# A graph message passing on one core: a slot pair's sum added in two halves instead of in one piece

## The chip, the core and the metric

The kernel runs on one core of a Trainium2 chip. The metric is the device time of one execution in microseconds; for each kernel several runs are timed and their median is given. The engines are named as the profile names them: PE (TensorE, with PEld for its weight loads), DVE (VectorE), ACT (ScalarE), POOL (GpSimd) and SP (SyncE, which here only issues transfers). "q" behind a name (DVEq) is the engine's queue.

## What is computed

A network of two layers on 1250 nodes with 512 features, each layer a message passing over 20000 edges followed by a block with attention and expert or plain feed-forward parts. The change lies in the message passing of the second layer. Cut to what matters:

```python
x0, x1 = lin(node_feats)                     # 128 scalars and 128 vectors of 3 a node
h = three layers of silu on edge_feats       # 64 values an edge
w1, w2, w3, w4 = split(h @ W_mlp4 / 8, 4)    # 4 x 128 weights an edge
s0, s1 = x0[sender], x1[sender]
p1 = w1 * s0 * y0                            # y0, y1: the edge's attributes
p2 = (w2 * s0)[:, :, None] * y1[:, None, :]
p3 = w3[:, :, None] * s1 * y0[:, None, :]
p4 = w4 * einsum('eum,em->eu', s1, y1) / SQRT3
msg0 = segment_sum(concat([p1, p4]), receiver, num_nodes)
msg1 = segment_sum(concat([p2, p3]), receiver, num_nodes)
out = lin(msg0, msg1) / 10
```

An edge's message has 1024 values (p1 and p3: 4 x 128, with the factor y0; p2 and p4: 4 x 128). The sum over the edges of a receiving node is what the changed lines add up.

## The kernel before

The program is a row of stages. Each stage (`stage`, L70) runs one block for each engine and ends in a barrier of all engines. The stage of interest is the first of `graph_sum1` (L2150), which runs from about 1362 to 1787 us of the span; the stage behind it turns `acc` and multiplies it with the output weights.

The edges are sorted by receiver into 176 slots of 128 edges (NS1), so that the two slots of a pair (88 pairs, PAIRS) belong to the same tile of 125 nodes. Which tile that is stands in `tile_base`, and is read at run time. `acc` (`g_acc`) holds 10 tiles of 1024 columns in SBUF.

For each slot, numbered i, j, t or s after the step at which an engine takes it:

- SP loads `h` (`g_h`) for 16 slots at a time, three buffers. POOL gathers the sending nodes' rows (`got`, L2208, 10 buffers) and makes `plain`, the 0/1 matrix of edge against receiver (L2216, 6 buffers), when `summed` says that PE is done with the slot six before. Once, in its step 9, POOL clears `acc` (L2219).
- PE makes the weights w1 to w4 of slot s in PSUM (`pw`, L2234, two matmuls).
- ACT makes the first part of the dot product (L2264), `hot` = `plain` times y0 (L2272) and three of the message's eight parts (L2281, signals `made_scaled`). `hot` has 4 buffers (MR), so L2272 for slot i waits for `summed` of slot i-4.
- DVE makes the rest: L2295 and L2310 (dot product, slot s), L2304, L2314, L2318 (message, slot s-1). `msg` has 4 buffers as well; L2302 and L2303 wait for `summed` and `made_scaled` of the slot four before.
- PE sums slot t = s-4 over the receivers: L2245 multiplies `hot` with the message's first 512 columns, L2248 `plain` with the other 512. Each is float32 and shows as two passes with a weight load each. The first slot of a pair opens two PSUM banks of `pm`, the second adds to them and closes them, and `summed` counts the slots done. `pm` has four banks, so two pairs are in flight.
- DVE adds a closed pair to its tile of `acc`: in every second step it reads the tile's number (L2323, `value_load`), waits for `summed` (L2324) and for its own last add (L2328), and adds the 1024 columns of two banks in one instruction (L2330), which signals `added`.
- Before a pair q opens its banks, PE waits at L2244 until pair q-2 is added.

Each engine works through its instructions in the order of the program; in a step s of DVE that order is L2295 (s), L2304 (s-1), L2310 (s), L2314 and L2318 (s-1), and in odd steps from 7 on L2330 for pair (s-7)/2. In a step s of PE it is L2234 (s), L2245 and L2248 (s-4).

The first message passing (`graph_sum0`'s loop in `first_layer`) has an add of the same kind, L1578: 125x512 from PSUM into a slice whose place is read at run time, with the making of a `hot` tile (L1566) behind it.

Of the kernel before, what the change touches and what calls it, by code (L numbers as in the profile page):

```python
# [22 lines left out]
ALU = mybir.AluOpType  # L23
# [4 lines left out]
D = 512  # L28
TN = 125
# [6 lines left out]
PAIRS = (E + NT * (2 * TE - 1)) // (2 * TE)  # L36
NS1 = 2 * PAIRS
# [2112 lines left out]
def graph_sum1(nc, c, table_d, tile_base, nodes_d, h_d, w4_d, out0_d, out1_d, x):  # L2150
# [4 lines left out]
    with ExitStack() as ctx:  # L2155
        sb = lambda name, shape, dt=F32: ctx.enter_context(nc.sbuf_tensor(f"{name}_{nc.next_id()}", shape, dt))
        acc = sb("g1_acc", [TN, NT, 2 * D])
        wo = sb("g1_wo", [128, 2, 2, 128])
        with ExitStack() as inner:
# [11 lines left out]
            pm = inner.enter_context(nc.psum_tensor(f"g1_pm_{nc.next_id()}", [128, 4, 512], F32))  # L2171
            table = table_d.rearrange("(p t) c -> p t c", p=128)
            with stage(nc, "edges_in", "w4_in", "w4_high", "w4_low", "wo_in", "zeroed", "made_plain", "made_hot", "weighed",
# [5 lines left out]
                @block.sync  # L2179
                def _(sp):  # L2180
                    def load(g):
                        if g >= HR:

                            sp.wait_ge(weighed, G1E * (g - HR + 1))
                        sp.dma_start(h[:, g % HR, :].bitcast(F32), h_d[g, :, :]).then_inc(h_in[g % HR], 16)

                    sp.dma_start(edges[:, :, :], table).then_inc(edges_in, 16)
                    for n in range(2):
                        sp.dma_start(w4[64 * n:64 * n + 64, :], w4_d).then_inc(w4_in, 16)
                    for g in range(HR):  # L2190
                        load(g)
                    for n in range(2):
                        sp.dma_start(wo[:, 0, n, :], out0_d[128 * n:128 * n + 128, :]).then_inc(wo_in, 16)
                        sp.dma_start(wo[:, 1, n, :], out1_d[128 * n:128 * n + 128, :]).then_inc(wo_in, 16)
                    for g in range(HR, GROUPS):
                        load(g)
                    sp.wait_ge(wo_in, 64)
# [23 lines left out]
                @block.tensor  # L2221
                def _(pe):
                    pe.wait_ge(w4_high, 1)
                    pe.wait_ge(w4_low, 1)
                    for s in range(NS1 + 4):
                        if s < NS1:
                            g, r = s // G1E, s % G1E
                            if r == 0:
                                pe.wait_ge(h_in[g % HR], 16 * (g // HR + 1))
                            if s >= 4:  # L2230

                                pe.wait_ge(made_msg, s - 3)
                            for n in range(2):
                                ins = pe.matmul(pw[:, s % 4, :], h[:, g % HR, TE * r:TE * r + TE], w4_two[:, n, :],  # L2234
                                                start=(n == 0), stop=(n == 1))
                            ins.then_inc(weighed, 1)
                        t = s - 4
                        if t < 0:
                            continue
                        q, second = t // 2, t % 2  # L2240
                        pe.wait_ge(made_hot, t + 1)
                        pe.wait_ge(made_msg, t + 1)
                        if q >= 2 and not second:
                            pe.wait_ge(added, q - 1)  # L2244
                        pe.matmul(pm[0:TN, 2 * (q % 2), :], hot[:, t % MR, :],  # L2245
                                  msg[:, t % MR, 0:4, :].rearrange("p a b -> p (a b)"), start=not second, stop=bool(second))
                        pe.wait_ge(made_scaled, t + 1)
                        pe.matmul(pm[0:TN, 2 * (q % 2) + 1, :], plain[:, t % OR, :],  # L2248
                                  msg[:, t % MR, 4:8, :].rearrange("p a b -> p (a b)"), start=not second, stop=bool(second))\
                            .then_inc(summed, 1)  # L2250
# [34 lines left out]
                @block.vector  # L2285
                def _(dve):
                    dve.wait_ge(w4_high, 1)
                    dve.tensor_tensor(w4_two[:, 1, :], w4[:, :], w4_two[:, 0, :].bitcast(F32), ALU.subtract)\
                        .then_inc(w4_low, 1)
                    dve.wait_ge(edges_in, 16)  # L2290
                    for s in range(NS1 + 7):
                        i = s
                        if i < NS1:
                            dve.wait_ge(dot0, i + 1)
                            dve.scalar_tensor_tensor(dot[:, i % MR, :], got[:, i % GR, 256:384], edges[:, i, 6:7],  # L2295
                                                     dot[:, i % MR, :], ALU.mult, ALU.add).then_inc(dot1, 1)
                        i = s - 1
                        if 0 <= i < NS1:
                            dve.wait_ge(weighed, i + 1)
                            if i >= MR:  # L2300

                                dve.wait_ge(summed, i - MR + 1)  # L2302
                                dve.wait_ge(made_scaled, i - MR + 1)  # L2303
                            dve.tensor_tensor(msg[:, i % MR, 0::8, :], pw[:, i % 4, 0:256].rearrange("p (a u) -> p a u", a=2),  # L2304
                                              got[:, i % GR, 0:128].unsqueeze(1).to_broadcast((128, 2, 128)), ALU.mult)\
                                .then_inc(made_own, 1)
                        i = s
                        if i < NS1:
                            dve.wait_ge(dot1, i + 1)
                            dve.scalar_tensor_tensor(dot[:, i % MR, :], got[:, i % GR, 384:512], edges[:, i, 7:8],  # L2310
                                                     dot[:, i % MR, :], ALU.mult, ALU.add).then_inc(dot2, 1)
                        i = s - 1
                        if 0 <= i < NS1:
                            dve.tensor_tensor(msg[:, i % MR, 1:4, :],  # L2314
                                              pw[:, i % 4, 256:384].unsqueeze(1).to_broadcast((128, 3, 128)),
                                              got[:, i % GR, 128:512].rearrange("p (m u) -> p m u", m=3), ALU.mult)
                            dve.wait_ge(dot2, i + 1)
                            dve.tensor_tensor(msg[:, i % MR, 7, :], pw[:, i % 4, 384:512], dot[:, i % MR, :], ALU.mult)\  # L2318
                                .then_inc(made_msg, 1)
                        t = s - 6  # L2320
                        if t >= 0 and t % 2:
                            q = t // 2
                            at = dve.value_load(tile_base[0:1, q:q + 1], min_val=0, max_val=NT - 1)  # L2323
                            dve.wait_ge(summed, t + 1)  # L2324
                            if q == 0:
                                dve.wait_ge(zeroed, 1)
                            else:
                                dve.wait_ge(added, q)  # L2328
                            dst = acc[:, bass.ds(at, 1), :].rearrange("p a b -> p (a b)")
                            dve.tensor_tensor(dst, dst, pm[0:TN, 2 * (q % 2):2 * (q % 2) + 2, :].rearrange("p a b -> p (a b)"),  # L2330
                                              ALU.add).then_inc(added, 1)
                    dve.wait_ge(added, PAIRS)

        acc_t = sb("g1_acct", [128, 2, 8, TN])
        p8 = ctx.enter_context(nc.psum_tensor(f"g1_pt_{nc.next_id()}", [128, 4, 512], F32))
# [218 lines left out]
```

## Time and profile before

| | |
|---|---|
| median of 3 runs | 3323.68 us (3322.3 to 3328.46) |
| the profiled execution | 3329.74 us, span 3327.9 us |
| mean granted clock of TensorE | 0.949 |
| PE busy, share of the span | 2957.0 us, 89% |
| DVE busy, share of the span | 2030.3 us, 61% |
| ACT busy, share of the span | 1465.1 us, 44% |
| POOL busy, share of the span | 944.3 us, 28% |

The profiled execution is one run; its span goes from the first to the last instruction, and its own time is 1.8 us longer. Shares of busy time are means over all stages. Matmul records carry modelled ends and overlap each other, so PE's starts tell more than its busy time. In a timeline, the bracket behind a row gives the idle time of that engine just before and the event that came last before the start.

### The profile page before, as it was taken

The numbers are of one execution on the slowest core, as the hardware profiler recorded it, in microseconds if no ns is written. First come the engines' busy times: TensorE is split into PE (matmuls) and PEld (weight loads), VectorE is DVE, ScalarE is ACT, GpSimd is POOL, SyncE is SP. The second block draws the span as 40 slices with busy tenths as digits, with TensorE's granted clock in tenths as the row PEclk, the third lists the DMA queues.
The fourth block names the chain that finished last, engine by engine and source line by source line (L and its number), as shares of the span: only waits on it lengthen the run. The fifth ranks groups of instructions, "written<-read, shape, count | busy, mean of one in ns | idle before, by whom it ended". The sixth has DMA issues, their size and how long they took to land. (4 is left out here: it accounts for less than half of the span.)

```text
span 3327.9 us, 47565 instructions
## 1 busy us (share of the span) xinstructions
PE 2957.0 (89%) x15718; PEld 2057.7 (62%) x15718; DVE 2030.3 (61%) x4335; ACT 1465.1 (44%) x3160; POOL 944.3 (28%) x994
## 2 busy tenths in 40 slices
PE   5978789998589968699998888989999899998898
PEld 3522287776557644244445665568777687776787
DVE  8989746776421126599996345652777537776444
ACT  1000035665135426466664345533666436664322
POOL 2057664671134330566661000000000000001210
PEclk9999999999689979799999899989999999999899
DMA  3047765331559953544441453226431154311322
GB/s 99 13 142 206 199 154 133 63 74 41 166 179 341 340 172 141 195 137 140 137 126 57 162 143 77 50 68 189 87 71 25 25 189 91 79 25 39 104 82 82
DMA packets 222607, 402.70 MB, mean 121 GB/s; under 512 B 44222, under 2 KB 140626, under 8 KB 218526
## 3 DMA queue, kind: packets, MB, share of 16 engines
q1 hardware_dynamic: 170866, 262.09, 27.7%
q0 software_dynamic: 49744, 134.92, 14.6%
q10 hardware_dynamic: 1756, 2.64, 0.3%
q8 instruction: 130, 2.13, 0.3%
q14 instruction: 111, 0.91, 0.1%
HBM read 315.84 MB, written 87.71 MB: 121 GB/s over the span
## 5 line engine op out<-in xcount | busy, mean ns | idle before, releaser
L904 ACT ACTIVATE at_p<-at_pb,at_max 125x1250 f32<-125x1250 f32 (+4 forms) x320 | 383.8, 1199 | 301.9 <-DVE at_unused L975 273.5
L790 PE MATMUL at_pb<-ident,at_p 125*125 125x125 f32 x2880 | 433.0, 281 | 20.0 <-ACT at_p L904 17.0
L790 PEld LDWEIGHTS at_pb<-ident,at_p 125*125 125x125 f32 x2880 | 390.2, 190 | 83.0 <-ACT at_p L904 22.3
L807 PE MATMUL at_pb<-at_pt,at_v 125*64 125x250 f32 x2880 | 355.7, 384 | 5.2 <-DVE s_t L1008 3.0
L968 DVE TENSOR_REDUCE at_wide<-at_pb 125x1 f32<-125x1024 f32 x240 | 293.6, 1224 | 21.0 <-PE at_pb L773 2.7
L890 ACT ACTIVATE at_pt<-at_pb 125x500 f32<-125x500 f32 (+1 forms) x448 | 232.8, 520 | 96.3 <-PE at_pb L790 91.9
L807 PEld LDWEIGHTS at_pb<-at_pt,at_v 125*64 125x64 f32 x2880 | 188.6, 137 | 104.0 <-issue 14.4
L750 PE MATMUL at_pb<-at_s,at_shared 128*128 128x500 f32 (+1 forms) x1152 | 229.3, 361 | 23.4 <-ACT at_shared L852 23.4
L986 DVE COPY at_pt<-at_pb 125x500 f32<-125x500 f32 (+1 forms) x416 | 232.3, 582 | 21.6 <-PE at_pb L790 21.6
L975 DVE TENSOR_SCALAR_CACHE_REDUCE at_unused<-at_pb,at_wide 125x226 bf16<-125x226 f32 x240 | 107.8, 449 | 204.7 <-PE at_pb L773 201.7
L750 PEld LDWEIGHTS at_pb<-at_s,at_shared 128*128 128x128 f32 x1152 | 196.0, 194 | 56.4 <-ACT at_shared L852 24.2
L712 POOL TENSOR_TENSOR s_t<-s_t,at_all 128x500 f32<-128x500 f32 (+1 forms) x33 | 42.9, 1300 | 648.8 <-DVE s_t L1008 648.6
L695 POOL DMA_INDIRECT table<-rows,slots x160 | 198.2, 1239 | 96.5 <-issue 87.5
L1452 PE MATMUL so_ps<-g_got,g_hot 128*125 128x512 f32 x332 | 177.5, 637 | 46.3 <-issue 11.9
L2208 POOL DMA_INDIRECT g_got<-nodes,g_edges x176 | 176.8, 1005 | 134.7 <-DMA g_edges<-table 104.4
L1404 POOL DMA_INDIRECT g_got<-support,so_ids x166 | 161.5, 973 | 149.8 <-DVE so_ids L1532 98.1
L2234 PE MATMUL g_pw<-g_w4two,g_h 128*128 128x512 f32 x352 | 182.1, 601 | 22.3 <-DMA g_h<-h_edges 18.5
L2245 PE MATMUL g_pm<-g_msg,g_hot 128*125 128x512 f32 x352 | 188.3, 617 | 14.9 <-DVE g_acc L2330 7.8
L771 PE MATMUL at_pb<-at_kh,at_q 128*125 128x512 f32 (+5 forms) x448 | 178.4, 405 | 19.5 <-ACT at_p L904 17.7
L2248 PE MATMUL g_pm<-g_msg,g_plain 128*125 128x512 f32 x352 | 181.5, 597 | 0.0
L771 PE MATMUL at_pb<-at_shared 128*125 128x512 f32 (+5 forms) x448 | 177.5, 403 | 3.3 <-ACT at_p L904 2.6
L1881 DVE COPY mo_y<-mo_py 78x512 f32<-78x512 f32 x64 | 44.0, 687 | 213.7 <-PE mo_py L1849 148.4
(336 smaller groups left out, 5695.1 us busy)
## 6 DMA issues: line engine op xcount, KB each, us to landing
w_ring<-in_L_ffn_w SPq DMA_DIRECT2D x128, 512.0 KB, 11.5
at_shared<-k_parts SPq DMA_DIRECT2D x64, 312.5 KB
ml_w<-in_mlp_w SPq DMA_DIRECT2D x64, 256.0 KB
k_parts<-at_shared SPq DMA_DIRECT2D x64, 250.0 KB, 2.9
q_parts<-at_shared SPq DMA_DIRECT2D x64, 250.0 KB, 2.8
h_edges<-em_both SPq DMA_DIRECT2D x11, 1024.0 KB, 4.1
g_h<-h_edges SPq DMA_DIRECT2D x11, 1024.0 KB, 5.7
at_shared<-q_parts SPq DMA_DIRECT2D x32, 312.5 KB
```

Source lines behind the costliest of these rows:

```text
L695: pool.indirect_dma_start(table_d, bass.IndirectOffsetOnAxis(ap=slots[:, t:t + 1], axis=0), rows[:, t, :], None).then_inc(sent, 16)
L750: ins = pe.matmul(bank[:, (x + 6) % 8, 0:s.stop - s.start], a[:, ci % 2, k, 128 * (j % 2):128 * (j % 2) + 128], b[:, k, s], start=(t == 0) ...
L771: pe.matmul(score[u % 2][0:TN, a:b], q_two[j % 2][h][:, TN * i:TN * i + TN], k_hi[j % 2][h][:, a:b], start=True, stop=False)
L790: ins = pe.transpose(pturn[0:TN, g % 2, TN * (t % 4):TN * (t % 4) + TN], p[:, u % 2, TN * t:TN * t + TN], c.ident[0:TN, 0:TN])
L807: ins = pe.matmul(pout[side:side + 64, 0:2 * TN], v[:, t, 2 * j + h, :], p_t[:, q % 2, t, :], start=(t < 2), stop=(t >= keys[u] - 2))
L890: act.activation(p_t[:, u // 2 % 2, 4 * n:4 * n + m, TN * (u % 2):TN * (u % 2) + TN], pturn[0:TN, g % 2, 0:TN * m].rearrange("p (a b) -> p ...
L904: act.activation(p[:, t % 2, 0:w], score[t % 2][0:TN, 0:w], ACT.Exp, bias=neg_max[:, t:t + 1], accum_out=total[:, t:t + 1]).then_inc(exp_d ...
L968: dve.tensor_reduce(neg_wide[:, u:u + 1], score[u % 2][0:TN, a:a + 1024], AX, ALU.max, negate=True)\
L986: dve.tensor_copy(p_t[:, u // 2 % 2, 4 * n:4 * n + m, TN * (u % 2):TN * (u % 2) + TN], pturn[0:TN, g % 2, 0:TN * m].rearrange("p (a b) -> ...
L2234: ins = pe.matmul(pw[:, s % 4, :], h[:, g % HR, TE * r:TE * r + TE], w4_two[:, n, :], start=(n == 0), stop=(n == 1))
L2245: pe.matmul(pm[0:TN, 2 * (q % 2), :], hot[:, t % MR, :], msg[:, t % MR, 0:4, :].rearrange("p a b -> p (a b)"), start=not second, stop=bool ...
L2248: pe.matmul(pm[0:TN, 2 * (q % 2) + 1, :], plain[:, t % OR, :], msg[:, t % MR, 4:8, :].rearrange("p a b -> p (a b)"), start=not second, sto ...
```

## The change

The pair's sum is added in two instructions of 512 columns, the first half in the even step of DVE and the second half in the odd one behind it, each behind its own reading of the tile's number. `added` counts halves. PE waits for the first half of pair q-2 before L2245 and for the second half before L2248. DVE's loop is one step shorter, since the last pair's halves fall into its steps NS1+4 and NS1+5.

```diff
                         if q >= 2 and not second:
-                            pe.wait_ge(added, q - 1)
+                            pe.wait_ge(added, 2 * (q - 2) + 1)
                         pe.matmul(pm[0:TN, 2 * (q % 2), :], hot[:, t % MR, :],
...
                         pe.wait_ge(made_scaled, t + 1)
+                        if q >= 2 and not second:
+                            pe.wait_ge(added, 2 * (q - 2) + 2)
                         pe.matmul(pm[0:TN, 2 * (q % 2) + 1, :], plain[:, t % OR, :],
...
-                    for s in range(NS1 + 7):
+                    for s in range(NS1 + 6):
...
                         t = s - 6
-                        if t >= 0 and t % 2:
-                            q = t // 2
+                        if t >= 0:
+                            q, half = t // 2, t % 2
                             at = dve.value_load(tile_base[0:1, q:q + 1], min_val=0, max_val=NT - 1)
-                            dve.wait_ge(summed, t + 1)
+                            if half == 0:
+                                dve.wait_ge(summed, 2 * q + 2)
                             if q == 0:
                                 dve.wait_ge(zeroed, 1)
                             else:
-                                dve.wait_ge(added, q)
-                            dst = acc[:, bass.ds(at, 1), :].rearrange("p a b -> p (a b)")
-                            dve.tensor_tensor(dst, dst, pm[0:TN, 2 * (q % 2):2 * (q % 2) + 2, :].rearrange("p a b -> p (a b)"),
-                                              ALU.add).then_inc(added, 1)
-                    dve.wait_ge(added, PAIRS)
+                                dve.wait_ge(added, 2 * (q - 1) + half + 1)
+                            dst = acc[:, bass.ds(at, 1), D * half:D * half + D].rearrange("p a b -> p (a b)")
+                            dve.tensor_tensor(dst, dst, pm[0:TN, 2 * (q % 2) + half, :], ALU.add).then_inc(added, 1)
+                    dve.wait_ge(added, 2 * PAIRS)
```

## Rows read from the trace of the kernel before

**Rows 1.** Windows: stretch, its us, busy us (x instructions) by engine, PE clock, DMA.
```profile
1600.00:1650.00 50.00, 49.12 (x130) 23.36 (x129) 45.47 (x119) 33.38 (x107) 34.43 (x43) 1.00 0.45 133
```

**Rows 2.** Timeline: start us, us, engine and line; adds of pairs 2, 84, 87.
```profile
1393.63 1.21 DVE L2330 TENSOR_TENSOR g_acc<-g_acc,g_pm 125x1024 f32 x1
...
1777.03 1.21 DVE L2330 TENSOR_TENSOR g_acc<-g_acc,g_pm 125x1024 f32 x1
...
1785.63 1.22 DVE L2330 TENSOR_TENSOR g_acc<-g_acc,g_pm 125x1024 f32 x1 [2.21 <-PE g_pm L2248]
```

**Rows 3.** Timeline of one pair of slots in the steady state.
```profile
1602.78 0.42 DVE L2304 TENSOR_TENSOR g_msg<-g_pw,g_got 128x256 f32<-128x256 f32 x1 [0.41 <-issue]
1602.78 0.40 ACT L2272 ACTIVATE g_hot<-g_plain,g_edges 128x125 f32<-128x125 f32 x1 [0.92 <-PE g_pm L2248]
...
1603.38 0.55 DVE L2314 TENSOR_TENSOR g_msg<-g_pw,g_got 128x384 f32<-128x384 f32 x1
...
1603.85 0.28 DVE L2318 TENSOR_TENSOR g_msg<-g_pw,g_dot 128x128 f32<-128x128 f32 x1
...
1604.05 1.21 DVE L2330 TENSOR_TENSOR g_acc<-g_acc,g_pm 125x1024 f32 x1
...
1604.97 0.40 ACT L2272 ACTIVATE g_hot<-g_plain,g_edges 128x125 f32<-128x125 f32 x1 [0.62 <-PE g_pm L2248]
...
1605.17 0.35 DVE L2295 SCALAR_TENSOR_TENSOR g_dot<-g_got,g_edges,g_dot 128x128 f32<-128x128 f32 x1
...
1605.37 0.29 PEld L2245 LDWEIGHTS g_pm<-g_msg,g_hot 128*125 128x125 f32 x2 [0.47 <-ACT g_hot L2272]
...
1605.44 0.42 DVE L2304 TENSOR_TENSOR g_msg<-g_pw,g_got 128x256 f32<-128x256 f32 x1
...
1606.77 0.19 PEld L2234 LDWEIGHTS g_pw<-g_w4two,g_h 128*128 128x128 f32 x1 [0.24 <-issue]
...
1607.45 0.42 DVE L2304 TENSOR_TENSOR g_msg<-g_pw,g_got 128x256 f32<-128x256 f32 x1 [0.41 <-issue]
...
1608.95 0.19 PEld L2234 LDWEIGHTS g_pw<-g_w4two,g_h 128*128 128x128 f32 x1 [0.24 <-DVE g_msg L2318]
```

**Rows 4.** Timeline at the stage's start and near its end: adds, L2272 and PE's loads.
```profile
1381.76 1.21 DVE L2330 TENSOR_TENSOR g_acc<-g_acc,g_pm 125x1024 f32 x1
1382.32 0.40 ACT L2272 ACTIVATE g_hot<-g_plain,g_edges 128x125 f32<-128x125 f32 x1 [0.28 <-POOL g_plain L2216]
...
1383.08 0.49 PEld L2245 LDWEIGHTS g_pm<-g_msg,g_hot 128*125 128x125 f32 x2 [8.21 <-ACT g_hot L2272]
...
1384.09 0.33 PEld L2248 LDWEIGHTS g_pm<-g_msg,g_plain 128*125 128x125 f32 x1 [0.52 <-ACT g_msg L2281]
...
1772.35 1.22 DVE L2330 TENSOR_TENSOR g_acc<-g_acc,g_pm 125x1024 f32 x1
...
1773.23 0.40 ACT L2272 ACTIVATE g_hot<-g_plain,g_edges 128x125 f32<-128x125 f32 x1 [0.61 <-PE g_pm L2248]
...
1773.68 0.29 PEld L2245 LDWEIGHTS g_pm<-g_msg,g_hot 128*125 128x125 f32 x2 [0.52 <-ACT g_hot L2272]
```

**Rows 5.** Timeline of DVE in the first message passing.
```profile
330.96 0.69 DVE L1578 TENSOR_TENSOR x_sb<-x_sb,so_ps 125x512 f32 x1 [0.25 <-PE so_ps L1452]
331.56 0.40 DVE L1566 TENSOR_SCALAR g_hot<-iota,so_near,so_by 128x125 f32<-128x125 f32 x1
```

**Rows 6.** Queue instructions by line: duration ns min/median/max, first and last start us.
```profile
L2323 DVEq TENSOR_LOAD <-base x1: 306/306/306, 1602.9 to 1602.9; - x1
...
L2330 DVEq FUSED_REGOPS  x1: 57/57/57, 1603.6 to 1603.6; - x1
...
L2244 PEldq EVENT_SEMAPHORE  x86: 51/51/51, 1383.0 to 1780.4; - x86
```

**Rows 7.** Waits between 1395 and 1780 us: total us, times, longest us.
```profile
ACT g_hot L2272 <- PE g_pm L2248: 126.5, 164, 1.0
POOL g_plain L2216 <- PE g_pm L2248: 95.5, 161, 1.9
```

## The prediction

> **What bounds the kernel now.** The page's busy shares are a mean over stages that end in a barrier of all engines, so I looked for what sets the pace inside the second message passing. A stretch of 50 us in its middle shows PE busy 49.12 of 50 us at a granted clock of 1.00 (the 2.4 GHz level) and DVE 45.47 [rows 1]. PE's ends are modelled, so this does not mean that PE is at its limit: starts must be used. The adds at L2330 give the pace. Pair 2's add starts at 1393.63, pair 84's at 1777.03 [rows 2]: 383.40 us for 82 pairs, 4.676 us for a pair of slots.
>
> The timeline of one pair [rows 3] shows that its two slots differ. PE's first weight load of a slot (L2234) stands at 1606.77 and 1608.95, 2.18 us for the slot that closes a pair; the one that opens a pair takes the rest, 4.676 - 2.18 = 2.49. It loses 0.31 us ahead of L2245, whose weights are loaded at 1605.37. The bracket there names ACT L2272, which ends at 1605.37. That is the last event, not the reason: L2272 starts when the slot four before its own has left its `hot` buffer, so it makes a tile that PE wants three slots later. What PE waits for by the code is L2244: `added` for the pair that had the same banks, and the add that signals it runs from 1604.05 to 1605.26, 0.11 before the load. Two other places part the candidates [rows 4]. In the first, the load at 1383.08 comes 0.11 after the end of the add (1381.76 + 1.21) and 0.36 after the end of L2272 (1382.32 + 0.40). In the second, near the end, the load at 1773.68 is again 0.11 after the add (1772.35 + 1.22), and 0.05 after L2272 (1773.23 + 0.40).
>
> Why is the add late? DVE idles 0.41 us ahead of L2304 at 1602.78 [rows 3]. The bracket says issue; but ACT L2272 starts at the same 1602.78, released by PE L2248, and L2304 waits for the same event (L2302: the message buffer is free). I call such a moment T: 1602.78, 1604.97, 1607.45. From T, DVE does L2304, L2310, L2314, L2318, and 1.27 later the add of 1024 columns. So a pair is a loop: T to the add's end 2.48, 0.11 to PE's load, then four passes (L2245 and L2248, two each) to the next T at 1607.45, 2.08. Together 4.67, the pace. PE's own work is 2 x 2.18 = 4.36.
>
> **The change, part by part.**
>
> 1. The wait of L2245. After the change it asks for the first half of pair q-2, which DVE adds one step earlier. The first half ends at T + 1.27 + 0.69 (the duration is below) of the step two before PE's; the second ends at T + 1.96 too, of the step one before. With slots of 2.18, L2245 then has over 2 us to spare; L2248, which comes one L2234 and two passes later, has about 1.3. The loop through the add is gone. Gain: 4.676 - 4.36 = 0.316 us a pair. The two-decimal starts are good to 0.01 a slot, so I take 0.305, 82 x 0.305 = 25 us.
>
> 2. The add in halves. The same form, 125x512 f32 from PSUM into a slice with a register offset, stands in the first message passing: it takes 0.69 us, and the next instruction starts 0.60 after it (330.96 to 331.56) [rows 5]. A 1024 add holds DVE 1.12 (1604.05 to 1605.17) [rows 3], so a pair costs DVE 2 x 0.60 - 1.12 = 0.08 more. DVE's slot, start to start: 1.27 from L2304 to the add, 0.60 for the half, 0.27 for L2295 (1605.17 to 1605.44) = 2.14, against PE's 2.18. DVE has 0.04 left, so this costs nothing on the path; it is the closest race here. Ends: no less than 0.47, what the 384-column L2314 holds DVE (1603.38 to 1603.85), no more than 0.69 unhidden. The latter makes a DVE slot of 2.23, which loses 0.10 a pair again, 8 us. I take 0.60, the same form's own row.
>
> The rows show an instruction that starts before its forerunner has ended: L2330 at 1604.05, while L2318 runs from 1603.85 for 0.28 [rows 3]. The Trainium skill's page "VectorE: DVE Perf Modes", section "The DRAIN you can't avoid", says that the next operation does not start until the pipe has emptied, and its rules ask for fewer operations. Read as "starts only after the end", it would make the kernel some 48 us slower where the rows make it 26 faster; the trace's starts contradict that reading.
>
> 3. The register. `value_load` (L2323) now comes in every step, not every second. Its chain on DVE's queue begins with TENSOR_LOAD, 306 ns at 1602.9, and ends with a register step of 57 ns at 1603.6 [rows 6]: it starts 0.1 after L2304 and is done 0.4 before the add could start at 1604.05. The four instructions ahead of the add hide it: cost 0. With that cover gone it would cost up to its 0.77 us a slot (a rival, below).
>
> 4. The new wait on PE before L2248, 86 times. The standing one at L2244 takes 51 ns [rows 6]. PE's loads have 0.24 idle ahead of each (1606.77) [rows 3], which hides it: cost 0; unhidden 0.05 x 86 = 4.4 us. DVE's waits before the halves are met when reached: L2302 asks for the same `summed` value earlier in the step, and the same half of the pair before was done two steps back. Nothing new is queued on ACT, POOL or SP. ACT waits for PE 126.5 us in 164 waits, POOL 95.5 in 161 [rows 7], 0.77 and 0.59 a slot, and the mean slot shrinks by 0.16, so neither becomes late. The gathers and the loads of `g_h` lose 7% of their lead; nothing waits for them in the stretch.
>
> 5. The start. PE's loads stand idle 8.21 us until 1383.08, behind the clearing of `g_acc` on POOL and the add of pair 0 [rows 4]. With the change the first half of pair 0 goes right behind the clearing, L2245 runs early, and L2248, now loaded at 1384.09, waits only for the second half: 1381.76 + 0.69 + 0.11 = 1382.56, 1.5 earlier. PE still runs slowly there, and when its clock rises is open: 0 to 2 us gained, I take 1.5.
>
> 6. The end. The last pair's add starts at 1785.63 [rows 2]. Its two halves have nothing between them that hides the second one's register chain, so they end about 0.1 + 0.77 + 0.69 = 1.6 after it, where the one add took 1.22: 0.4 lost.
>
> **Sum**: -25 - 1.5 + 0.4 = -26.1 us. Nothing of the next stage overlaps the loop, so the span shortens by all of it. The profiled execution took 3329.74 us (span 3327.9), which gives 3303.6. It stood 6.1 above the median of the runs, 3323.68, which gives 3297.6; I say 3297.5. What a measurement can tell from no change here is about 0.2%, 6.6 us.
>
> **Rivals.**
>
> *DVE becomes the bound.* If the halves hold DVE 0.69 instead of 0.60, or the waits between them show, a pair takes 2 x 2.23 = 4.46: the gain is 0.216 x 82 = 17.7 and 1.1 at the ends, 3304.9. For it: only 0.04 us of slack. Against it: 330.96 to 331.56 [rows 5].
>
> *Nothing changes* (3324). The bracket at 1605.37 would be right and ACT's `hot` the wait. Against it stand the two places of [rows 4] and the count of buffers. A milder form, that with `added` gone `hot`, the message or the gather holds PE instead, fails on ACT's 0.77 and POOL's 0.59 a slot.
>
> *Slower: the register chain is exposed.* If its 0.77 us began only when L2318 has ended, the half would start at T + 1.07 + 0.28 + 0.77 = T + 2.12, not T + 1.27, in every slot. DVE's slot would be 2.14 + 0.85 = 2.99, a pair 5.98, and the kernel 82 x (5.98 - 4.676) = 107 us slower, 3431. It decides from the point where DVE's slot passes 2.34, 0.20 above my sum. The load at 1602.9 speaks against it [rows 6]: it runs while L2304 runs.
>
> *Slower: no overlap between DVE's instructions.* The durations in full are 0.42 + 0.35 + 0.55 + 0.28 + 0.69 + 0.35 = 2.64 a slot, 5.28 a pair, near 82 x 0.59 = 48 us slower, 3372. The starts in [rows 3] exclude it unless the new order brings a hold that the trace does not have.
>
> **How the numbers follow.** Forecast 0.83; DVE the bound 0.07; nothing changes 0.05; register chain exposed, wholly or in part, 0.04; no overlap 0.01. Faster by over 0.2%: 0.90; within 0.2%: 0.05; slower: 0.05. The low end of the range takes 0.316 a pair (26), 2 at the start, and 3 us for the scatter of the runs (3322.3 to 3328.46): 3292. The high end takes the DVE-bound case and 3 of scatter: 3307.5, which also holds PE's new wait unhidden (3302).
>
> **What would show it.** Right: adds of 512 columns x176 at about 0.69 us, a pace of 4.37 a pair, every slot 2.18 between L2234's first loads, DVE's idle ahead of L2304 down to 0.05, and PE's first stop ending in L2248 near 1382.6. Steps wrong: a pair at 4.46 with L2304 never idle (DVE the bound); TENSOR_LOAD starting after L2318 (register); a slot still at 2.49 with the stop ahead of L2245 (not `added`). The forecast as a whole falls if the second halves hold PE as the whole add did, or if another stage changes by more than 3 us.

## The result, and the profile after

| | before | after |
|---|---|---|
| median of the runs on one chip | 3326.07 us (3322.3 to 3331.56) | 3299.66 us (3297.24 to 3302.92) |
| ratio, 95% interval | | 0.992 (0.9901 to 0.9938) |
| span of the profiled execution | 3327.9 us | 3296.2 us |
| first load of `g_h` to the end of the last add | 440.1 us | 410.5 us |

The change saves 26.4 us by the medians; 26.1 were forecast. The time came out at 3299.66 us where 3297.5 was forecast, and the kernel before stood 2.4 us higher in these runs than in those that the forecast started from. The stage itself is 29.6 us shorter in the profiles. Four rows of the stage in the profile after (lines behind the diff have moved: L2297, L2306, L2312, L2316, L2320 are the former L2295, L2304, L2310, L2314, L2318; L2250 the former L2248, L2274 and L2283 ACT's L2272 and L2281, L2325 the reading of the tile's number, L2333 the add; L2249 is PE's new wait):

```profile
1345.55 0.59 SPq L2185 DMA_DIRECT2D g_h<-h_edges  x1
...
1387.29 0.68 DVE L2333 TENSOR_TENSOR g_acc<-g_acc,g_pm 125x512 f32 x1
...
1745.01 0.67 DVE L2333 TENSOR_TENSOR g_acc<-g_acc,g_pm 125x512 f32 x1
...
1754.59 1.46 DVE L2333 TENSOR_TENSOR g_acc<-g_acc,g_pm 125x512 f32 x2 [1.96 <-PE g_pm L2250]
```

They show SP's first load of the stage, the first half of pair 2, the first half of pair 84, and the last pair's two halves. Between the second and the third lie 357.72 us, 4.362 us a pair, against 4.676 in [rows 2]: 82 x 0.313 = 25.7 us. The kernel before issued its first load at 1346.76, 1.2 us later in its span than this one; no changed work lies ahead of it:

```profile
1346.76 0.59 SPq L2185 DMA_DIRECT2D g_h<-h_edges  x1
```

One pair of slots in the steady state, the answer to [rows 3]:

```profile
1601.03 0.19 PEld L2234 LDWEIGHTS g_pw<-g_w4two,g_h 128*128 128x128 f32 x1 [0.24 <-issue]
...
1601.69 0.42 PEld L2245 LDWEIGHTS g_pm<-g_msg,g_hot 128*125 128x125 f32 x2
1601.72 0.40 ACT L2274 ACTIVATE g_hot<-g_plain,g_edges 128x125 f32<-128x125 f32 x1 [0.61 <-PE g_pm L2250]
1601.72 0.63 POOL L2216 TENSOR_SCALAR g_plain<-iota,g_edges 128x125 f32<-128x125 f32 x1
1601.84 0.41 DVE L2297 SCALAR_TENSOR_TENSOR g_dot<-g_got,g_edges,g_dot 128x128 f32<-128x128 f32 x1
...
1602.17 0.41 DVE L2306 TENSOR_TENSOR g_msg<-g_pw,g_got 128x256 f32<-128x256 f32 x1
...
1603.22 0.19 PEld L2234 LDWEIGHTS g_pw<-g_w4two,g_h 128*128 128x128 f32 x1 [0.24 <-issue]
...
1603.43 0.67 DVE L2333 TENSOR_TENSOR g_acc<-g_acc,g_pm 125x512 f32 x1
...
1603.88 0.42 PEld L2245 LDWEIGHTS g_pm<-g_msg,g_hot 128*125 128x125 f32 x2
...
1604.03 0.39 DVE L2297 SCALAR_TENSOR_TENSOR g_dot<-g_got,g_edges,g_dot 128x128 f32<-128x128 f32 x1
...
1604.54 0.19 PEld L2250 LDWEIGHTS g_pm<-g_msg,g_plain 128*125 128x125 f32 x1 [0.24 <-issue]
...
1605.39 0.19 PEld L2234 LDWEIGHTS g_pw<-g_w4two,g_h 128*128 128x128 f32 x1 [0.24 <-issue]
```

PE's first load of a slot stands at 1601.03, 1603.22 and 1605.39: the two kinds of slot now take 2.19 and 2.17, 2.18 in the mean of the stage, and no bracket stands before L2245. The window says the same of the engine (columns as in [rows 1]):

```profile
1600.00:1650.00 50.00, 50.00 (x139) 25.84 (x138) 50.00 (x139) 35.98 (x116) 37.34 (x47) 1.00 0.54 164
```

139 matmul records in 50 us, where [rows 1] have 130: the same work at 1.07 times the pace. DVE too is at 50.00, which the last section takes up. The start of the stage, against [rows 4]:

```profile
1375.54 0.69 DVE L2333 TENSOR_TENSOR g_acc<-g_acc,g_pm 125x512 f32 x1 [4.76 <-POOL g_acc L2219]
1376.35 0.29 PEld L2245 LDWEIGHTS g_pm<-g_msg,g_hot 128*125 128x125 f32 x2 [2.62 <-issue]
...
1380.34 0.68 DVE L2333 TENSOR_TENSOR g_acc<-g_acc,g_pm 125x512 f32 x1
...
1381.13 0.50 PEld L2250 LDWEIGHTS g_pm<-g_msg,g_plain 128*125 128x125 f32 x2 [4.49 <-ACT g_msg L2283]
```

The first half goes right behind POOL's clearing and L2245 runs; PE then stops once more, ahead of L2250, until 0.11 after the end of the second half (1380.34 + 0.68). Counted from SP's first load, L2250 starts at 35.58 us, before at 37.33 (1384.09 - 1346.76): 1.75 earlier.

### The profile page after: what moved, and what is told of

It is laid out like the page before. It is cut to its first block and busy times, and to the rows that moved or that the text cites. A ratio compares the mean times of both kernels' runs of the same rounds, so it can differ in the third digit from the quotient of the medians.

```text
span 3296.2 us, 48091 instructions
## 1 busy us (share of the span) xinstructions
PE 2932.8 (89%) x15718; PEld 2060.1 (62%) x15718; DVE 2036.8 (62%) x4423; ACT 1465.3 (44%) x3160; POOL 940.6 (29%) x994
## 5 line engine op out<-in xcount | busy, mean ns | idle before, releaser
L2208 POOL DMA_INDIRECT g_got<-nodes,g_edges x176 | 176.4, 1002 | 133.8 <-DMA g_edges<-table 103.6
L2234 PE MATMUL g_pw<-g_w4two,g_h 128*128 128x512 f32 x352 | 181.8, 600 | 22.5 <-DMA g_h<-h_edges 18.3
L2250 PE MATMUL g_pm<-g_msg,g_plain 128*125 128x512 f32 x352 | 181.6, 598 | 3.7 <-DVE g_acc L2333 3.7
L2245 PE MATMUL g_pm<-g_msg,g_hot 128*125 128x512 f32 x352 | 180.7, 595 | 2.2 <-DVE g_acc L2333 2.2
```

What stands on the lines that cost most here:

```text
L2245: pe.matmul(pm[0:TN, 2 * (q % 2), :], hot[:, t % MR, :], msg[:, t % MR, 0:4, :].rearrange("p a b -> p (a b)"), start=not second, stop=bool ...
```

## The experiments

The first theory, as predicted: PE waited ahead of L2245 for the add of the pair that had its banks, and add, PE's four passes and DVE's wait for a free message buffer formed a loop of 4.67 us; with the loop under 4.36, PE's own work sets the pace. The rivals: the wait is for ACT's `hot`; or it is the split, with a wait for each half, that gains.

| kernel | median, us | ratio to before (95%) | us a pair | stage, us |
|---|---|---|---|---|
| e1_hot6 | 3325.02 | 0.9999 (0.999 to 1.0009) | 4.672 | 438.6 |
| e2_early_whole | 3294.39 | 0.9906 (0.9889 to 0.9922) | 4.328 | 406.6 |
| e3_late_halves | 3295.57 | 0.9913 (0.9896 to 0.9929) | 4.357 | 411.4 |
| e4_one_wait | 3298.02 | 0.9917 (0.9898 to 0.9935) | 4.352 | 411.1 |
| e5_rings6 | 3299.3 | 0.9929 (0.9907 to 0.9951) | 4.365 | 412.0 |
| e6_spare | 3332.77 | 1.0024 (1.0014 to 1.0034) | 4.761 | 443.8 |
| e7_clear_dve | 3291.18 | 0.9901 (0.9882 to 0.992) | 4.343 | 400.3 |
| f1_whole_clear | 3288.39 | 0.9883 (0.9868 to 0.9898) | 4.350 | 402.2 |
| f2_pool_fill | 3295.35 (one run) | | 4.357 | 407.2 |
| f3_changed | 3302.35 | 0.9928 (0.9914 to 0.9942) | 4.352 | 410.1 |

Each ratio is to runs of the kernel before on the same chip, whose medians lie between 3324.10 and 3324.83 us. "us a pair" is the time from pair 2's first add to pair 84's, by 82; "stage" goes from SP's first load of `g_h` to the end of the last add.

**e1_hot6: is it `hot`?** The kernel before, with

```diff
-            hot = sb2("g1_hot", [128, MR, TN])
+            hot = sb2("g1_hot", [128, OR, TN])
...
-                            if i >= MR:
-                                act.wait_ge(summed, i - MR + 1)
-                            act.activation(hot[:, i % MR, :], ...
+                            if i >= OR:
+                                act.wait_ge(summed, i - OR + 1)
+                            act.activation(hot[:, i % OR, :], ...
```

> The kernel before with six `hot` buffers instead of four and nothing else; the add stays whole and in the odd step. Loop theory (PE waits ahead of L2245 for the add of the pair that had its banks): nothing changes, 4.676 us a pair, time within 0.2% of the kernel before. Rival (the wait is for ACT's `hot`, as the bracket at 1605.37 says): the wait goes, up to 0.31 us a pair, 25 us, about 3300.

Nothing changes. Its timeline around an opening slot, which now also parts the two candidates in the middle of the stage:

```profile
1601.93 1.21 DVE L2330 TENSOR_TENSOR g_acc<-g_acc,g_pm 125x1024 f32 x1
...
1602.31 0.39 ACT L2272 ACTIVATE g_hot<-g_plain,g_edges 128x125 f32<-128x125 f32 x1
...
1603.26 0.29 PEld L2245 LDWEIGHTS g_pm<-g_msg,g_hot 128*125 128x125 f32 x2 [0.48 <-issue]
```

L2272 is done at 1602.70, 0.56 before the load. The load comes 0.12 after the add's end at 1603.14, and the bracket names nobody now. The rival falls: in the kernel before, L2272's end stood next to the load because both follow from PE's summing: L2272 starts at one T, and the add ends 2.48 us after the T before it.

**e2_early_whole, e3_late_halves, e4_one_wait: which part of the change gains?** Three kernels that each keep one part. e2 (from the kernel before) moves the whole add one step earlier:

```diff
-                    for s in range(NS1 + 7):
+                    for s in range(NS1 + 6):
...
-                        if t >= 0 and t % 2:
+                        if t >= 0 and t % 2 == 0:
...
-                            dve.wait_ge(summed, t + 1)
+                            dve.wait_ge(summed, t + 2)
```

> The add stays whole (1024 columns, one wait on PE) but stands in DVE's even step, one step earlier, as the first half does after the change. Loop theory: what counts is when the banks are given back. The add ends 2.2 us earlier against PE, the loop is gone, 4.36 us a pair, about 26 us faster than before, as the change. DVE works 2.66 in one step and 1.53 in the other, 4.19 a pair, still under PE. Rival (it is the split, two short adds with waits of their own, that gains): 4.68 a pair, no change.

e3 (from the changed kernel) adds both halves in the odd step:

```diff
-                        if t >= 0:
-                            q, half = t // 2, t % 2
+                        if t >= 0 and t % 2:
+                            q = t // 2
...
+                            for half in range(2):
+                                dst = acc[:, bass.ds(at, 1), D * half:D * half + D]...
+                                dve.tensor_tensor(dst, dst, pm[0:TN, 2 * (q % 2) + half, :], ALU.add).then_inc(added, 1)
```

> Two halves with two waits on PE, but both in the odd step, where the whole add stood. Loop theory: the first half ends at T + 1.27 + 0.69 = T + 1.96 instead of T + 2.48; the loop is 1.96 + 0.11 + 2.08 = 4.15, less than PE's 4.36, so PE is the bound again: 4.36 a pair, about 25 us faster. Rival (only the earlier step helps): 4.68. DVE's work is the same 4.26 a pair.

e4 (from the changed kernel) waits once on PE:

```diff
                         if q >= 2 and not second:
-                            pe.wait_ge(added, 2 * (q - 2) + 1)
+                            pe.wait_ge(added, 2 * (q - 2) + 2)
...
-                        if q >= 2 and not second:
-                            pe.wait_ge(added, 2 * (q - 2) + 2)
```

> The changed kernel, but PE waits for both halves in one wait ahead of L2245. Loop theory: the second half ends at T + 1.96, the loop through it is again 1.96 + 0.11 + 2.08 = 4.15, under PE's 4.36: the same time as the changed kernel, 4.36 a pair, no 0.1 us lost. Only at the start is it slower, since L2245 waits with L2248: under 2 us. Rival (the halves must be awaited each by itself): the 0.31 us ahead of L2245 come back in part, 4.5 to 4.7 a pair.

All three are as fast as the change, or faster by no more than these runs can tell: each takes the loop under 4.36 us, and below that it does not matter by how much. The split alone does it, because a half is done 0.54 us sooner (1.21 against 0.67 us, e3), and the earlier step alone does it (e2). With one wait on PE for both halves the pace is the same (e4); at the start, the second bank of pair 2 is opened later: L2248's load comes 36.30 us after SP's first load, and the same load 35.58 and 35.18 us after it in the two profiles of the changed kernel. Two rows of each for the pace, from the timelines of e2, e3 and e4 in this order:

```profile
1387.95 1.20 DVE L2330 TENSOR_TENSOR g_acc<-g_acc,g_pm 125x1024 f32 x1
...
1742.82 1.21 DVE L2330 TENSOR_TENSOR g_acc<-g_acc,g_pm 125x1024 f32 x1
```

```profile
1390.42 0.67 DVE L2333 TENSOR_TENSOR g_acc<-g_acc,g_pm 125x512 f32 x1
...
1747.66 0.68 DVE L2333 TENSOR_TENSOR g_acc<-g_acc,g_pm 125x512 f32 x1
```

```profile
1386.10 0.67 DVE L2331 TENSOR_TENSOR g_acc<-g_acc,g_pm 125x512 f32 x1
...
1742.94 0.68 DVE L2331 TENSOR_TENSOR g_acc<-g_acc,g_pm 125x512 f32 x1
```

e2's 4.328 is a little below PE's 4.35 because pair 2's add is still late behind the start there. It has the shortest stage of the three: its first add gives back both banks right behind the clearing. Of the 4.5 to 4.8 us by which it is shorter, 0.9 us lie ahead of anything that differs: ACT makes the weights 5.59 us after SP's first load there, and 6.45 us after it in e3 and e4.

**e5_rings6: cut the loop at its other edge.** The kernel before, with one number changed:

```diff
-    HR, GR, MR, OR, AHEAD = 3, 10, 4, 6, 5
+    HR, GR, MR, OR, AHEAD = 3, 10, 6, 6, 5
```

> The kernel before with six buffers each for the message, `hot` and the dot product; the add stays whole and in the odd step. This cuts the loop at its other edge: L2304 no longer waits for the slot four before, so DVE may start its step some 1.8 us before T. Loop theory: the add is early by that, PE never waits for it, 4.36 a pair, about 25 us faster. Rival (the add in that step is too late whatever DVE waits for, or the split is what gains): 4.68.

The add is untouched, in one piece, in its old step, and the pace is 4.365: the wait of L2304 for a message buffer was one edge of the loop, as the prediction read it from two equal start times. The edit widens three rings at once (message, `hot`, dot product). e1 excludes `hot`. No run widens the message ring by itself; against the dot product's ring stands [rows 3], where DVE's idle 0.41 us lie ahead of L2304, which does not read it, and not ahead of L2295, which does.

```profile
1387.70 1.20 DVE L2330 TENSOR_TENSOR g_acc<-g_acc,g_pm 125x1024 f32 x1
...
1745.59 1.21 DVE L2330 TENSOR_TENSOR g_acc<-g_acc,g_pm 125x1024 f32 x1
```

**e6_spare: how much has DVE left?** The changed kernel, with behind L2312 one more instruction of its form:

```diff
+                            dve.scalar_tensor_tensor(spare[:, :], got[:, i % GR, 384:512], edges[:, i, 7:8],
+                                                     got[:, i % GR, 256:384], ALU.mult, ALU.add)
```

> The changed kernel with one more DVE instruction of L2310's form in every step (a spare result that nobody reads). It measures what DVE has left. My sum: DVE's slot is 2.14 and gets 0.26 to 0.27 more, 2.40, over PE's 2.18: 4.80 a pair, 82 x 0.44 = 36 us slower than the changed kernel. If DVE had over 0.26 to spare a slot, the pace would stay at 4.36; if it had none, it would be 4.88 or more.

One step of DVE in its timeline (L2315 is the spare, L2336 the add):

```profile
1600.29 0.67 DVE L2336 TENSOR_TENSOR g_acc<-g_acc,g_pm 125x512 f32 x1
1600.88 0.33 DVE L2298 SCALAR_TENSOR_TENSOR g_dot<-g_got,g_edges,g_dot 128x128 f32<-128x128 f32 x1
1601.14 0.41 DVE L2307 TENSOR_TENSOR g_msg<-g_pw,g_got 128x256 f32<-128x256 f32 x1
1601.48 0.33 DVE L2313 SCALAR_TENSOR_TENSOR g_dot<-g_got,g_edges,g_dot 128x128 f32<-128x128 f32 x1
1601.74 0.33 DVE L2315 SCALAR_TENSOR_TENSOR g_spare<-g_got,g_edges 128x128 f32<-128x128 f32 x1
1602.00 0.54 DVE L2319 TENSOR_TENSOR g_msg<-g_pw,g_got 128x384 f32<-128x384 f32 x1
1602.47 0.27 DVE L2323 TENSOR_TENSOR g_msg<-g_pw,g_dot 128x128 f32<-128x128 f32 x1
1602.67 0.67 DVE L2336 TENSOR_TENSOR g_acc<-g_acc,g_pm 125x512 f32 x1
```

DVE is the bound: 2.38 us a slot, 0.26 of it the spare (1601.74 to 1602.00), the half 0.59. Without the spare, DVE needs 2.12 a slot where the sum said 2.14, and has 0.06 left under PE's 2.18. The slowdown shows that DVE was next in line: 0.40 a pair, 33 us in the stage, with 36 expected.

**e7_clear_dve, f1_whole_clear: the start.** The changed kernel's profile shows PE stopped twice behind the clearing. e7 moves it from POOL to DVE, which waits for the weights and the gathered rows then:

```diff
-                            pool.memset(acc[:, :, :], 0.0).then_inc(zeroed, 1)
...
+                    dve.memset(acc[:, 0:NT // 2, :], 0.0).then_inc(zeroed, 1)
                     dve.wait_ge(w4_high, 1)
                     dve.tensor_tensor(w4_two[:, 1, :], ...
+                    dve.memset(acc[:, NT // 2:NT, :], 0.0).then_inc(zeroed, 1)
```

> The changed kernel, but DVE clears `g_acc` in two pieces before and behind its work on the weights, while it waits for the first gathered rows, and POOL no longer does. In the changed kernel PE stands idle 2.2 and 3.7 us at the start behind POOL's 8.65 us of clearing, and its clock falls once more. Expected: both stops go, POOL makes `plain` every 1.84 us, and the kernel is 5 to 9 us faster than the changed one, about 3292; the steady pace stays 4.36. If DVE's clearing takes longer than its idle time (5.7 us between the weights and the first gathered rows), the first slots come later by the difference.

```profile
1343.97 4.33 DVE L2287 MEMSET g_acc<- 125x5120 f32 x1 [6.02 <-issue]
1350.73 0.69 DVE L2289 TENSOR_TENSOR g_w4two<-g_w,g_w4two 128x512 fp32r<-128x512 f32 x1 [2.43 <-ACT g_w4two L2255]
1352.44 4.33 DVE L2291 MEMSET g_acc<- 125x5120 f32 x1 [1.02 <-issue]
1356.68 0.23 DVE L2297 SCALAR_TENSOR_TENSOR g_dot<-g_got,g_edges,g_dot 128x128 f32<-128x128 f32 x1
```

Both pieces fit into DVE's idle time but for 0.4 us: ACT's part for the first L2297 is done at 1356.30, and L2297 starts at 1356.68. PE's granted clock stays at 1.00 from 1364 us to the end of the loop, where the changed kernel has 0.68 between 1376 and 1380 and 0.50 between 1380 and 1384, around its two stops. The stage is 10.2 us shorter than the changed kernel's, and the median 8.5 lower (against other runs of the kernel before, so this difference has the scatter of both). f1 puts e2 and e7 together.

> The whole add in the even step (as in e2_early_whole) and DVE clearing `g_acc` (as in e7_clear_dve) in one kernel. Loop theory: PE is the bound from the first slots on, 2.175 us a slot as in both; the start is that of e7_clear_dve, so the stage is within 1 us of that kernel's (400.3 us from the first load of `g_h` to the last add) and the time near 3290. If the halves are worth something of their own, it is slower than e7_clear_dve by that.

It gives 3288.39 us, against 3302.35 for the changed kernel (f3_changed) on the same chip, 14.0 us less, and is the fastest kernel of this study by its median; from e7 it cannot be told apart (3291.18, intervals that overlap). Its stage is 402.2 us, 1.9 more than e7's, where within 1 was expected: ACT makes the stage's weights 6.8 us after the first load where e7 has 5.7, ahead of anything that differs, and its slot is 2.178 instead of 2.175. So the halves are worth nothing of their own that these runs could show.

> The changed kernel again, on the same chip as f1_whole_clear, to place that one against it. Loop theory: a pace of 4.36 a pair; 3297 to 3300 us, 0.991 to 0.992 of the kernel before.

f3 is 0.9928 of the kernel before where 0.991 to 0.992 was expected, and 2.4 us above the upper end given, though its stage (410.1) is that of the first profile (410.5). What it has more lies outside the stage: behind the last add it runs 1544.9 us, the first profile 1540.2. No changed work lies there. Against its own runs of the kernel before it saves 22.5 us, where the first set of runs gave 26.4.

**f2_pool_fill: what stretches L2297?** It belongs to the last section. POOL's comparison is left out, so this kernel does not compute the sum.

```diff
-                            pool.tensor_scalar(plain[:, j % OR, :], c.iota[:, 0:TN], edges[:, j, 1:2], None, ALU.is_equal)\
+                            pool.memset(plain[:, j % OR, :], 1.0)\
```

> The changed kernel, but POOL fills `plain` with ones by a memset (no input read from SBUF) instead of comparing; the 0/1 matrix of receivers is left out of the computation. In the changed kernel L2297 (two inputs from SBUF) takes 0.40 to 0.41 us whenever it starts 0.10 to 0.11 after L2216, 0.35 otherwise. If the two instructions contend for reading SBUF, no L2297 takes over 0.36, wherever it starts, and DVE's start behind T does not stay at 0.43. If the 0.05 comes from PE or ACT, it stays where L2297 starts at that place. PE's pace stays 2.18 a slot in either case.

## Why the prediction was right, point by point

- *The wait of L2245 and the loop (forecast 25 us).* Right in mechanism and size: 25.7 us in 82 pairs. e1 excludes `hot`; e2 to e5 take the loop under PE's own work in four ways (an earlier step, a shorter add, both with one wait, and wider rings) and all come to 4.33 to 4.37 us a pair.
- *The add in halves.* Duration 0.674 us at the median against 0.69 expected; it holds DVE 0.60 us, as expected. DVE's slot is 2.12 by e6, so it is not the bound. The rival "DVE becomes the bound" was 0.06 us a slot away.
- *The time to spare of the second half (about 1.3 us).* Too large, with no effect on the sum. Before 1540 us L2250's load comes 0.87 us after the end of the second half, of which 0.11 is the way from the add to the load: 0.76 to spare. Behind 1540 us it is 0.44 (1603.43 + 0.67 to 1604.54 in the rows above), 0.33 to spare. For the first half, "over 2 us" is right (2.39 and 1.96, less 0.11).
- *The reading against overlap.* The full durations of a step (0.41, 0.34, 0.55, 0.28, 0.67 and 0.40) add up to 2.65 us, and a slot takes 2.18. Read strictly, the rule that the prediction took from the Trainium skill's page "VectorE: DVE Perf Modes", section "The DRAIN you can't avoid", does not hold for this order of instructions either. The same paragraph of that section goes on that a next operation which is not held starts earlier, and the prediction left that out; these rows agree with it, since each instruction starts 0.08 us before the recorded end of its forerunner. The rival's price had a slip: 5.28 - 4.676 is 0.60, not 0.59, so 82 pairs are 49.5 us and the time 3373, not 3372. In the same way the upper end of the range, 3304.9 and 3 of scatter, is 3307.9 and not 3307.5.
- *The register.* Hidden, as said: in the profile after, the load starts 0.13 behind L2306, and the half is not late. The part by line (columns as in [rows 6]):

```profile
L2325 DVEq TENSOR_LOAD <-base x1: 304/304/304, 1602.3 to 1602.3; - x1
```

- *The new wait on PE.* It is there 86 times, 51 ns each, and costs nothing that PE's slots show: e4 does without it and has 4.352 against 4.362, 0.8 us over the 82 pairs, the same spread as between two profiles of the changed kernel (4.352 and 4.362). It has a use that the prediction did not see: behind 1540 us L2245's load (1603.88) comes 0.22 before the end of the second half (1604.10), and only because it asks for the first half alone does PE not wait there.

```profile
L2249 PEldq EVENT_SEMAPHORE  x86: 51/51/51, 1381.1 to 1750.1; - x86
```

- *The start (forecast 1.5 us).* Right in kind, too small in size. L2250 starts 1.75 earlier within the stage, and the difference grows to 2.9 us two slots later: between 1384 and 1388 us the granted clock is 0.97 after and 0.50 before. The stage's 29.6 us are 25.7 in steady state, and 3.9 at both ends.
- *The end (forecast 0.4 lost).* The last pair's halves take 1.46 us where the one add took 1.22, so 0.24 was lost: the second half's register chain starts 0.03 us behind the first half (1754.61), where 0.1 was allowed, and the second half follows the first by 0.78, where 0.87 was. More than that was won back where I had left it out: in the kernel before PE's loads stand idle 1.34 us ahead of L2245 at 1778.35, and in the last slots after no idle time ahead of a load is over 0.31.
- *The total.* 26.1 forecast, 26.4 by the medians, 29.6 in the stage, 31.7 in the spans. The spans contain 1.2 ahead of the stage and 0.9 behind it, where nothing was changed. Executions of one kernel differ by 6 to 9 us, and the other set of runs (f3) gives 22.5 saved, so the near match of 26.1 and 26.4 is in part luck. By the profile the sum was 3.5 us too small: 0.7 in the loop, and 2.8 in the start and the end.

## What to carry to other kernels

Where two engines pass buffers in a ring, add up one whole round (wait, work, signal, work, signal) and compare it with each engine's own work: only a loop that is longer than the busiest engine's work costs anything. Here it could be cut by a shorter instruction, by an earlier one, or by more buffers. The bracket at a wait names the last event, which can be a neighbour tied to the same event further back; widen that neighbour's ring, or look at the start and end of the stage where the ties differ. After such a cut, look at the next engine: here DVE had 0.06 us a slot to spare.

## What the runs showed that was not expected

DVE is busy 50.00 of 50 us, though its work is 2.12 us a slot and the slot is 2.18. The share cannot show that slack: each record reaches 0.08 us past the start of the next instruction, which is more than the 0.06 us of waiting. So it is 50.00 in the first half of the loop too (columns as in [rows 1]), and f2, below, has 200.00 of 200 us:

```profile
1400.00:1450.00 50.00, 50.00 (x139) 25.82 (x138) 50.00 (x139) 35.98 (x116) 36.98 (x46) 1.00 0.51 156
```

What the timeline does show is a lag that DVE does not make up. Up to 1540, L2306 starts with T but for a few slots at the start. Then it comes 0.35 late once, and from there on 0.43 behind T in every slot:

```profile
1538.23 0.35 DVE L2297 SCALAR_TENSOR_TENSOR g_dot<-g_got,g_edges,g_dot 128x128 f32<-128x128 f32 x1
1538.55 0.42 DVE L2306 TENSOR_TENSOR g_msg<-g_pw,g_got 128x256 f32<-128x256 f32 x1
...
1541.07 0.42 DVE L2306 TENSOR_TENSOR g_msg<-g_pw,g_got 128x256 f32<-128x256 f32 x1 [0.32 <-issue]
...
1543.01 0.42 DVE L2297 SCALAR_TENSOR_TENSOR g_dot<-g_got,g_edges,g_dot 128x128 f32<-128x128 f32 x1
1543.35 0.41 DVE L2306 TENSOR_TENSOR g_msg<-g_pw,g_got 128x256 f32<-128x256 f32 x1
```

With 0.06 to spare a slot the delay should be made up in about seven slots. It is not, because L2297 now starts 0.10 behind POOL's L2216 (1542.91) and takes 0.40 to 0.42 instead of 0.35, which eats what was spare. f2, where POOL's L2216 reads nothing from SBUF, has the same late start (0.35 behind T), but has made it up six slots later, by 0.06 a slot. e4, with POOL's instruction unchanged, makes it up as well, and its timeline shows by what: after two late slots one slot of PE is longer (2.38 us instead of 2.18), so L2295 there starts ahead of L2216, takes 0.34, and the lag falls from 0.43 to 0.17, 0.10, 0.04 and 0. The longer slot is e4's one wait: its L2245 asks for the second half too, and is loaded 0.12 behind the end of that (L2331 is the add there).

```profile
1540.87 0.67 DVE L2331 TENSOR_TENSOR g_acc<-g_acc,g_pm 125x512 f32 x1
...
1541.66 0.29 PEld L2245 LDWEIGHTS g_pm<-g_msg,g_hot 128*125 128x125 f32 x2 [0.37 <-issue]
```

The lag is kept only while nothing moves the two instructions against each other. L2297 between 1540 and 1740 us, in the changed kernel and in f2 (duration min/median/max):

```profile
L2297 DVE SCALAR_TENSOR_TENSOR g_dot<-g_got,g_edges,g_dot x92: 348/400/417, 1540.4 to 1739.1; 128x128 f32<-128x128 f32 x92
```

```profile
L2297 DVE SCALAR_TENSOR_TENSOR g_dot<-g_got,g_edges,g_dot x92: 336/344/348, 1541.6 to 1739.6; 128x128 f32<-128x128 f32 x92
```

The reading that fits these rows is that a DVE instruction with two inputs from SBUF is held up by a POOL instruction that has just begun to read there, here by some 0.06 us. The Trainium skill's page "SBUF — State Buffer", section "SBUF: two separate sides", tells of a port pair that the two engines share, and says that whoever starts first has it for the whole instruction and the other is blocked fully. The trace agrees that they contend, and not on that length: L2216 runs 0.61 us, L2297 loses 0.06, and in [rows 3] L2295 starts 0.20 behind T, while L2216 runs, and takes its usual 0.35. Nor is 0.06 the most that is lost. At the start of the stage after, an L2312 that starts 0.09 behind L2216 takes 0.44 us instead of 0.34, and the L2297 behind it takes 0.55:

```profile
1364.29 0.62 POOL L2216 TENSOR_SCALAR g_plain<-iota,g_edges 128x125 f32<-128x125 f32 x1
1364.38 0.44 DVE L2312 SCALAR_TENSOR_TENSOR g_dot<-g_got,g_edges,g_dot 128x128 f32<-128x128 f32 x1
...
1365.41 0.55 DVE L2297 SCALAR_TENSOR_TENSOR g_dot<-g_got,g_edges,g_dot 128x128 f32<-128x128 f32 x1
```

In f2 none of these instructions takes over 0.38 us. What the 0.55 come from stays open; no L2216 runs beside that one, and a gather of POOL (L2208) does in f2 as well, where the L2297 at 1362.87 takes 0.33. f2's POOL instruction in the loop is also shorter (0.20 us), and once it has caught up DVE hardly starts at that place any more, so f2 does not tell whether POOL's reading, its length or only the place makes the difference. The delay was harmless in the changed kernel, as the second half still had 0.33 us to spare; what holds L2306 back once, at the same slot in the changed kernel, f2, e4 and f3, stays open.
